# Ordering an eight-stage attention pipeline so that TensorE's fp32 instructions stand in four stretches a batch

## What is computed

```python
for W in (layer0, layer1):
    q = x @ Wq + bq;  k = ctx @ Wk + bk;  v = ctx @ Wv + bv
    w = softmax(q @ k.T / sqrt(512), axis=queries)
    y = w @ v + x
    x = (y - mean(y)) * rsqrt(var(y) + 1e-6) * gamma + beta
```

## Time and profile before

| | us |
|---|---|
| median of 3 runs | 1019.43 (1016.87 to 1020.06) |
| the profiled execution | 1016.79 |
| its span, first to last instruction | 1014.9 |
| mean granted TensorE clock | 0.995 |

### The profile page before, as it was taken

One profiled execution on the slowest core, in us unless ns is written; L12 is line 12 of the kernel. 1 busy time (PEld: TensorE's weight loads), 2 busy tenths in 40 slices (PEclk: granted clock), 3 DMA queues, 4 the chain that ended last, 5 costly groups with the idle time before them and its releaser, 6 DMA issues. The chain is left out here.

```text
span 1014.9 us, 23859 instructions
## 1 busy us (share of the span) xinstructions
PE 989.6 (98%) x6940; PEld 930.9 (92%) x6940; DVE 876.8 (86%) x2616; ACT 664.1 (65%) x1864; POOL 567.6 (56%) x522
## 2 busy tenths in 40 slices
PE   7989999999999999999999999999999999999985
PEld 6879999999999999999999999999999999999975
DVE  4788889988988998888988988898898889888867
ACT  2457767666766666776766676677667666667642
POOL 0134575556566555656555556655565665556574
PEclk9999999999999999999999999999999999999998
DMA  8653434544444454443454444345444445544101
GB/s 213 134 113 77 104 80 97 109 99 102 101 98 78 100 113 98 97 99 84 90 108 97 105 99 98 79 97 114 97 97 100 90 87 105 115 96 97 54 19 37
DMA packets 373958, 98.32 MB, mean 97 GB/s; under 512 B 308488, under 2 KB 357786, under 8 KB 373914
## 3 DMA queue, kind: packets, MB, share of 16 engines
q1 hardware_dynamic: 371370, 96.98, 44.2%
q10 hardware_dynamic: 2544, 0.80, 0.4%
HBM read 83.06 MB, written 14.68 MB: 96 GB/s over the span
## 5 line engine op out<-in xcount | busy, mean ns | idle before, releaser
L680 PE MATMUL oq_bank<-probs,raw 125*128 125x224 f32 x1488 | 302.8, 353 | 1.7 <-ACT probs L929 1.7
L680 PEld LDWEIGHTS oq_bank<-probs,raw 125*128 125x128 f32 x1488 | 272.2, 190 | 2.3 <-ACT probs L929 1.2
L913 ACT ACTIVATE probs<-probs,neg_max 125x224 f32<-125x224 f32 x378 | 177.8, 472 | 143.7 <-DVE neg_max L1194 143.6
L1521 POOL TENSOR_TENSOR psum<-probs 125x672 f32<-125x672 f32 x62 | 100.1, 1615 | 243.8 <-ACT probs L929 243.8
L656 PE MATMUL score_bank<-qT_hi,cT_hi 128*125 128x224 f32 x768 | 199.6, 286 | 3.9 <-ACT cT_hi L870 1.8
L657 PE MATMUL score_bank<-qT_hi,cT_lo 128*125 128x224 f32 x768 | 188.9, 273 | 0.0
L929 ACT ACTIVATE probs<-probs,rsum 125x224 f32<-125x224 f32 x378 | 150.8, 471 | 10.8 <-DVE rsum L1210 9.4
L1584 POOL TENSOR_TENSOR y_out<-z,gamma_row 112x512 f32<-112x512 f32 x62 | 93.9, 1536 | 113.9 <-ACT z L953 113.9
L656 PEld LDWEIGHTS score_bank<-qT_hi,cT_hi 128*125 128x125 f32 x768 | 145.2, 189 | 8.8 <-ACT cT_hi L870 3.4
L661 PE MATMUL score_bank<-qT_lo,cT_hi 128*125 128x224 f32 x768 | 147.1, 273 | 0.0
L657 PEld LDWEIGHTS score_bank<-qT_hi,cT_lo 128*125 128x125 f32 x768 | 145.4, 189 | 0.0
(11 more groups left out here) (136 smaller groups left out, 2038.9 us busy)
## 6 DMA issues: line engine op xcount, KB each, us to landing
raw<-in_ctx_dram SPq DMA_DIRECT2D x64, 375.0 KB
cb<-in_ctx_dram SPq DMA_DIRECT2D x248, 92.0 KB
x<-in_x_dram SPq DMA_DIRECT2D x32, 448.0 KB, 3.6
xb<-in_x_dram SPq DMA_DIRECT2D x124, 112.0 KB, 3.0
out_dram<-y_out SPq DMA_DIRECT2D x31, 448.0 KB, 6.7
cb<-in_ctx_dram SPq DMA_DIRECT2D x124, 3.5 KB
y<-in_L_xattn_Wq_dram SPq DMA_DIRECT2D x2, 512.0 KB, 5.5
Wq_next<-in_L_xattn_Wq_dram SPq DMA_DIRECT2D x2, 512.0 KB, 12.6
```

The source lines that it names most:

```text
L680: ins = nc.tensor.matmul(o, raw[0:MP, u.slot, c, cols], probs[0:MP, u.par4, c, :], start=(c == 0), stop=(c == MC - 1))
L913: ins = act.activation(probs[0:MP, u.par4, c, :], probs[0:MP, u.par4, c, :], ACT.Exp, bias=neg_max[0:MP, u.par4, c:c + 1], scale=-1.0, acc ...
```

## The change

Only the order of calls changes, on all five lists; no call is added or removed. TensorE's list, whole:

```diff
             def turn(i, j):
                 a, b = units(i, j)
+                spread_d(a(+0))
+                o_product(b(-1), 0)
                 score_product(a(+0), 0)
+                score_product(a(+0), 1)
+                transpose_x(b(+0), 0)
                 o_product(b(-1), 1)
-                transpose_x(b(+0), 0)
-                score_product(a(+0), 1)
+                transpose_x(b(+0), 1)
                 score_product(a(+0), 2)
-                transpose_x(b(+0), 1)
+                q_product(b(+0), 0)
                 pv_product(b(-1), 0)
-                q_product(b(+0), 0)
+                spread_d(b(+0))
+                q_product(b(+0), 1)
                 pv_product(b(-1), 1)
-                q_product(b(+0), 1)
-                o_product(a(+0), 0)
-                spread_d(b(+0))
                 score_product(b(+0), 0)
                 score_product(b(+0), 1)
+                o_product(a(+0), 0)
                 o_product(a(+0), 1)
                 score_product(b(+0), 2)
+                pv_product(a(+0), 0)
+                pv_product(a(+0), 1)
                 q_product(a(+1), 0)
-                pv_product(a(+0), 0)
-                spread_d(a(+1))
-                pv_product(a(+0), 1)
                 q_product(a(+1), 1)
-                o_product(b(+0), 0)
```

The fp32 stretches of a turn were o+r+transpose, transpose, o+spread, o+r, spread, o: six. They become spread+o, transpose+o+r+transpose, spread, o+o+r: four. VectorE's list, its first third (the calls behind are moved alike):

```diff
             def turn(i, j):
                 a, b = units(i, j)
+                score_max(b(-1), 2)
+                score_max(b(-1), 3)
+                ctxT_lo(a(+0), 0)
+                add_eps(b(-2))
+                turn_ctx(a(+0), 1)
                 shift(b(-2), 0)
-                score_max(b(-1), 2)
+                o_lo(a(-1), 0)
+                invert_sum(b(-1), 0)
                 shift(b(-2), 1)
-                dot(a(+0), 0)
-                dot(a(+0), 1)
+                o_lo(a(-1), 1)
                 residual(a(-1), 0)
                 residual(a(-1), 1)
-                score_max(b(-1), 3)
-                invert_sum(b(-1), 0)
-                o_lo(a(-1), 1)
+                ctxT_lo(a(+0), 1)
                 score_max(b(-1), 4)
+                turn_ctx(a(+0), 2)
                 score_max(b(-1), 5)
-                ctxT_lo(a(+0), 0)
                 add_pv(a(-1), 0)
+                add_pv(a(-1), 1)
+                half_moments(a(-1), 0)
+                invert_sum(b(-1), 1)
                 q_lo(a(+0), 0)
...
```

ScalarE's list, the calls around the second o_hi of a, and its end:

```diff
                 o_hi(a(-1), 1)
                 standardise(b(-2), 0)
+                ctxT_hi(a(+0), 1)
                 standardise(b(-2), 1)
-                ctxT_hi(a(+0), 0)
+                normalise(b(-1), 0)
+                ctxT_hi(a(+0), 2)
+                exps(b(-1), 1)
                 q_hi(a(+0), 0)
-                normalise(b(-1), 0)
-                exps(b(-1), 1)
                 normalise(b(-1), 1)
                 q_hi(a(+0), 1)
-                ctxT_hi(a(+0), 1)
-                o_hi(b(-1), 0)
+                d_out(a(+0))
+                standardise(a(-1), 0)
```

GpSimd's list and SP's:

```diff
+                inverse_deviation(a(-1))
                 sum_thirds(b(-1))
+                scale(a(-1), 0)
                 sum_two(b(-1))
-                inverse_deviation(a(-1))
                 sum_probs(b(-1))
-                scale(a(-1), 0)
-                add_beta(a(-1), 0)
-                scale(a(-1), 1)
                 sum_thirds(a(+0))
                 sum_two(a(+0))
+                scale(a(-1), 1)
+                add_beta(a(-1), 0)
+                sum_probs(a(+0))
+                inverse_deviation(b(-1))
                 add_beta(a(-1), 1)
-                inverse_deviation(b(-1))
-                sum_probs(a(+0))
                 scale(b(-1), 0)
...
                 if a(+0).later(1):
+                    load_xb(a(+0))
+                store(b(-3))
+                if a(-1).later(0):
+                    load_ctx(a(-1), 0)
+                    load_ctx(a(-1), 1)
+                if a(+0).later(1):
                     load_cb(a(+0))
                 if a(+1).later(1):
-                    load_xb(a(+1))
-                if a(+1).later(1):
                     load_x(a(+1))
-                if a(+0).later(0):
-                    load_ctx(a(+0), 0)
-                    load_ctx(a(+0), 1)
-                store(b(-2))
```

More of the change, by code:

```diff
@@ L767, in opening @@
                 spread_bk(1)
+                score_product(a1, 1)
                 transpose_x(b0, 0)
-                score_product(a1, 1)
+                transpose_x(b0, 1)
                 score_product(a1, 2)
-                transpose_x(b0, 1)
                 q_product(b0, 0)
+                spread_d(b0)
                 q_product(b0, 1)
-                o_product(a1, 0)
-                spread_d(b0)
                 score_product(b0, 0)
                 score_product(b0, 1)
+                o_product(a1, 0)
                 o_product(a1, 1)
                 score_product(b0, 2)
-                q_product(a2, 0)
                 pe.wait_ge(c_done, (LC + 1) * LAYERS)
                 pv_product(a1, 0)
-                spread_d(a2)
                 pv_product(a1, 1)
+                q_product(a2, 0)
                 q_product(a2, 1)
-                o_product(b0, 0)
             opening()
@@ L957, in turn @@
                 a, b = units(i, j)
-                ctxT_hi(a(-1), 2)
-                d_out(a(-1))
+                o_hi(b(-2), 0)
+                ctxT_hi(a(-1), 3)
                 if j is not None or i > 2:
-                    standardise(a(-2), 0)
                     standardise(a(-2), 1)
-                ctxT_hi(a(-1), 3)
+                xT_hi_part(b(-1), 0)
                 o_hi(b(-2), 1)
-                xT_hi_part(b(-1), 0)
-                exps(a(-1), 0)
                 xT_hi_part(b(-1), 1)
                 xT_hi_part(a(+0), 0)
+                exps(a(-1), 0)
                 exps(a(-1), 1)
@@ L1025, in _ @@
             q_hi(a1, 1)
+            ctxT_hi(a1, 2)
+            d_out(a1)
             turns(act, turn, 2)
@@ L1323, in turn @@
                 moments(a(-1), 1)
-                ctxT_lo(a(+0), 1)
+                add_eps(a(-1))
+                ctxT_lo(a(+0), 2)
+                turn_ctx(a(+0), 3)
+                shift(a(-1), 0)
                 q_lo(a(+0), 1)
[L1326 to L1329, removed]
                 shift(a(-1), 1)
-                ctxT_lo(a(+0), 2)
                 score_max(a(+0), 0)
-                turn_ctx(a(+0), 3)
@@ L1334, in turn @@
                 score_max(a(+0), 1)
                 ctxT_lo(a(+0), 3)
+                o_lo(b(-1), 0)
+                turn_x(a(+1), 0)
+                score_max(a(+0), 2)
                 xT_lo_part(b(+0), 0)
-                o_lo(b(-1), 1)
[L1338 to L1342, removed]
-                invert_sum(a(+0), 0)
-                score_max(a(+0), 5)
@@ L1345, in turn @@
-                xT_lo_part(b(+0), 1)
-                residual(b(-1), 1)
-                dot(b(+0), 0)
+                dot(b(+0), 0)
+                dot(b(+0), 1)
+                score_max(a(+0), 3)
+                residual(b(-1), 0)
+                xT_lo_part(b(+0), 1)
+                score_max(a(+0), 4)
+                score_max(a(+0), 5)
+                o_lo(b(-1), 1)
+                residual(b(-1), 1)
+                xT_lo_part(a(+1), 0)
+                invert_sum(a(+0), 0)
+                invert_sum(a(+0), 1)
@@ L1348, in turn @@
+                dot(a(+1), 0)
+                dot(a(+1), 1)
+                q_lo(b(+0), 0)
+                q_lo(b(+0), 1)
                 add_pv(b(-1), 0)
-                q_lo(b(+0), 0)
-                invert_sum(a(+0), 1)
-                dot(b(+0), 1)
+                turn_x(a(+1), 1)
                 half_moments(b(-1), 0)
-                xT_lo_part(a(+1), 0)
-                turn_x(a(+1), 1)
-                q_lo(b(+0), 1)
                 add_pv(b(-1), 1)
                 moments(b(-1), 0)
-                half_moments(b(-1), 1)
@@ L1431, in _ @@
             fold_c(1, 2)
+            turn_ctx(a1, 3)
             score_max(a1, 0)
-            turn_ctx(a1, 3)
             score_max(a1, 1)
             ctxT_lo(a1, 3)
+            turn_x(a2, 0)
+            score_max(a1, 2)
             xT_lo_part(b0, 0)
-            score_max(a1, 2)
+            dot(b0, 0)
+            dot(b0, 1)
             score_max(a1, 3)
-            turn_x(a2, 0)
+            xT_lo_part(b0, 1)
             score_max(a1, 4)
+            score_max(a1, 5)
+            xT_lo_part(a2, 0)
             invert_sum(a1, 0)
-            score_max(a1, 5)
-            xT_lo_part(b0, 1)
-            dot(b0, 0)
+            invert_sum(a1, 1)
+            dot(a2, 0)
+            dot(a2, 1)
             q_lo(b0, 0)
-            invert_sum(a1, 1)
-            dot(b0, 1)
-            xT_lo_part(a2, 0)
+            q_lo(b0, 1)
             turn_x(a2, 1)
-            q_lo(b0, 1)
-            o_lo(a1, 0)
             xT_lo_part(a2, 1)
@@ L1454, in _ @@
             score_max(b0, 1)
+            turn_ctx(a2, 0)
             Wv_lo_part(1)
-            turn_ctx(a2, 0)
             turns(dve, turn, 2)
```

14 lines of the change are left out of this document (5 added, 9 removed).

## The result

The changed kernel takes 1078.57 us (median, 1077.32 to 1079.16) against 1018.78, a ratio of 1.0586 with an interval of 1.0571 to 1.0602. I had said 1034, and 1014 to 1041. The direction is right, the size is not: 60 us, not 15.

The account below looks back on a forecast made before the run. TensorE's issue rate bounds the kernel; turns of 30.38 against 29.79 (7) and 30.41 against 29.915 (22) add 15.0 us, giving 1031.8, and 1034 with the median 2.6 us above the profiled execution. Range 1014 to 1041.

Parts of the forecast that it names:

- What bounds the kernel: TensorE runs at its own rate of issue, busy 989.6 of 1014.9 us; a new wait costs its full length.
- Fewer stretches: TensorE goes from six fp32 stretches a turn to four: 0.03 us a turn won, at most 0.18.
- The second rival: Each TensorE switch is worth the full 0.09 us, chain intact: 8.1 us less, 1011; chance 0.03.
- Loop waits: TensorE's two small waits in the loop, for oT_lo and before a score product, go: 0.13 us a turn won.
- The collision: GpSimd's scale holds VectorE's second residual about 1.05 us every turn; TensorE waits 0.62 to 0.65 at o_product(b, 0); chance 0.57.
- cb, "0 to 1 us a turn": In SP's queue cb starts near 8.6 us into the turn instead of 6.7; 0 to 1 us a turn, taken at nothing.
- The first: Rival: VectorE keeps its place between two residuals and GpSimd waits; the chain fits, 3.6 us less, 1016; chance 0.25.
- the third: Rival: without a collision, TensorE's wait on q_lo just misses by up to 0.15 us each turn, 1020; chance 0.11.
- The fourth: Rival: collision and late cb together, up to 1 us a turn more, near 1050; chance 0.04.
- Opening and tail: Both are reordered with the same work; put at 0, bound by 1 us each way.

Follow-up runs that it names:

- e8: The kernel before with ScalarE's ctxT_hi(a, 0) ahead of the two standardise(b-2), so GpSimd asks 0.4 us later: 1015.87 us, 0.9972.
- e6: The changed kernel with cb's transfers split around raw's second half, and ctxT_hi(a, 1) and normalise(b-1, 0) ahead of both standardise(b-2) on ScalarE: 1021.91 us, 1.0037.
- e5: The changed kernel with cb's transfers split, blocks 0 and 1 between the halves of raw, 2 and 3 behind them: 1041.89 us, 1.0228.
- e10: The kernel before with the changed kernel's order of SP's calls and nothing else: 1017.88 us, 0.9995.
- e2: The changed kernel with ctxT_hi(a, 1) and normalise(b-1, 0) ahead of the two standardise(b-2) on ScalarE, so GpSimd asks later: 1043.18 us, 1.0245.
- e4: The kernel before with o_lo(a-1, 1) ahead of the two residuals of a on VectorE, as in the changed kernel: 1027.46 us, 1.0094.
- e7: The kernel before with spread_d(a+1) moved to just ahead of o_product(b, 0), five fp32 stretches a turn instead of six: 1018.18 us, 1.0001.
- e9: The kernel of e6 with the opening's two transpose_x(b0) apart again, two score products between them: 1021.01 us, 1.0028.
- e1: The changed kernel with load_cb whole between the two halves of load_ctx in SP's list: 1050.97 us, 1.0322.
- e11: The kernel of e5 with VectorE's two residuals of a ahead of o_lo(a-1, 1), as in the kernel before: 1037.64 us, 1.0186.

## Why the prediction was right or wrong, step by step

**What bounds the kernel: right.** TensorE has no slack; 54.8 of the 62.2 us are in the turns, and the weight loads wait 46.8 us there at the one place named. Another 6.7 are the four stretches at the lower clock. My sum had no term for them: I had said that a new wait costs its full length, and four of these cost 1.67 us more.

**Fewer stretches, 0.03 us a turn: no gain.** 29.79 with six and with five, 29.81 with four. The second rival is dead. That agrees with my reading, that the delay behind an fp32 instruction is its own time, written to the next; the 0.015 that I still took was nothing.

**Loop waits, 0.13 a turn: about right.** e8 takes most of them away and wins 0.11 in undisturbed turns. In e6 they are gone too, but a few disturbed turns (mean 29.89, undisturbed ones 29.81) give it back.

**The collision: right in mechanism, place and size.** One residual of about 1.78 us in every turn, and GpSimd next each time: I had written 1.05 us of hold. By the Trainium skill, page "SBUF — State Buffer", section "Who interferes with whom", whoever issues first shuts the other out for that instruction. The trace agrees: between 909.11 and 911.60 above, both engines are slower than alone, the two scales with 3.46 us against 3.10 in the earlier trace rows, the two residuals with 2.49 against 1.34. Apart from cb it costs 0.65 us a turn in e5's mean; I had 0.62 to 0.65. In settled turns of the loop e5 takes 30.35 to 30.42 where I had 30.41, behind it 30.27 where I had 30.38, so there my stall was 0.1 too long.

**cb, "0 to 1 us a turn", taken at 0: this step failed.** Its first issue I had put 8.6 us into the turn, whose head is spread_d, 0.2 us ahead of o_product(b, 0), and it came nearly there. After, TensorE:

```profile
884.63 1.59 PE L680 MATMUL oq_bank<-probs,raw 125*128 125x224 f32 x7 [1.35 <-DVE qT_lo L1177]
```

and SP's queue:

```profile
893.22 3.33 SPq L388 DMA_DIRECT2D cb<-in_ctx_dram  x2
...
903.23 0.81 SPq L389 DMA_DIRECT2D cb<-in_ctx_dram  x1
```

893.22 - 884.63 = 8.6, and 8.8 with the spread. The user was wanted at 19.6. What I never put in the sum is how long twelve issues take: the last starts 903.23 - 893.22 = 10.0 us behind the first, and turn_ctx starts at 905.40, 12.2 us behind it. 8.8 + 12.2 = 21.0: 1.4 us late, which is the wait of 1.42. The trace of before had this length too. SP's queue before, the last issue of the turn of the earlier trace rows:

```profile
519.81 0.84 SPq L389 DMA_DIRECT2D cb<-in_ctx_dram  x1
```

and its user on VectorE:

```profile
521.88 0.59 DVE L1131 STREAM_TRANSPOSE t_bank<-cb 128x384 f32<-128x384 f32 x1 [0.17 <-DMA cb<-in_ctx_dram]
```

521.88 - 510.50 = 11.4 us from first issue to use, and a wait of 0.17 at its end: cb was already just in time. 8.6 + 11.4 = 20.0 against 19.6 would have told me that it is late, from before's rows alone. (The other 0.8 us of the 12.2 are the stretched first issues that e10 shows too; before's rows don't have them.) I read one row for the start of a load and none for its end.

**How the two add up.** My own numbers give it once cb is in. The late cb makes VectorE wait 41.2 / 21 = 1.96 us, of which the 0.7 us of idle that I had named covers a part: 1.26. The collision adds 1.05. The room ahead of o's weights was 1.05 - 0.62 = 0.43. Both: 1.26 + 1.05 - 0.43 = 1.88, measured 1.72 as wait at line 680 and as the difference of median turns; the mean's 1.91 has the lower clock in it. cb alone: 1.91 (40.2 / 21 in e2) - 0.7 - 0.43 = 0.78, measured 0.67 (0.74 by medians). The collision alone: 0.62, measured 0.65 (0.62). The turn quoted above has it in single steps: o_hi 0.65 late, plus 1.05, less 0.43, is 1.27; from the spread at 914.34 to the o at 915.75 it is 1.41, against 863.82 - 863.63 = 0.19 without a wait, 1.22 more. That the pieces fit within 0.2 us is an account and not a proof, but no other wait of size is left for it.

**The rivals.** The first is dead (e4), the second too (e7), the third had its condition but no case: without the collision q_lo just makes it (e6). The fourth was the right one, with a chance of 0.04 and 1050. It was too small in both: I bounded cb at 1 us, and it adds 31.79 - 30.54 = 1.25 to the collision, 0.23 of it by the lower clock; by median turns it is 31.53 - 30.43 = 1.10, and nothing softened it, since the room was spent.

**Opening and tail, 0, bound by 1 us each way: wrong.** 3.7 us each. In the opening it is in part the second transpose, 3.3 us, which e9 only moved. In the tail, 1.6 are the wait for q_lo once more, at the 30th o_product (1009.73), behind the 29 turns that I counted. The rest are after's waits on the matmuls (950 to 1080), of which these are the longest apart from those for q_lo (total, times, longest):

```profile
PE oq_bank L680 <- ACT probs L927: 1.7, 1, 1.7
PE oq_bank L636 <- DVE xT_lo L1146: 1.4, 1, 1.4
PE t_bank L590 <- ACT z L951: 1.3, 1, 1.3
PE score_bank L656 <- DVE neg_max L1194: 1.0, 1, 1.0
```

The kernel before waits for the same four there, only shorter (890 to 1015):

```profile
PE t_bank L590 <- DVE xT_lo L1146: 1.3, 1, 1.3
PE oq_bank L680 <- ACT probs L929: 0.8, 1, 0.8
PE t_bank L590 <- ACT z L953: 0.6, 1, 0.6
PE score_bank L656 <- DVE neg_max L1194: 0.4, 1, 0.4
```

5.4 against 3.1 us: the other 2 us or so. I had called it the same work; but where there is no next batch to fill in, a new order pays for each dependence whose ends it moves closer. That it is the order, and which call, was read from the rows and not tried.

**The sum with what was measured:** turns without either cause 29 x (29.89 - 29.90) = -0.5; the collision 29 x 0.65 = +18.9; cb on top of it 29 x 1.25 = +36.4; opening and tail +7.4. Together 62.2, the difference of the spans. It closes because each term is a difference of the same measured times, and is no check of the causes; of the 36.4, 6.7 are the lower clock.

## What to carry to other kernels

When a step that frees a buffer moves back, follow the transfer behind it to its last landing and not to its first issue, and set that against the moment its user is due; a wait of 0.1 or 0.2 us for a DMA in the old trace says that there is no slack. Two small delays that lean on the same room must be added before the room is taken off, once. A wait may cost more than its length: look at the granted clock behind it. And where GpSimd and VectorE meet over SBUF, look who triggers GpSimd: moving that trigger by a call or two cost nothing here, and even made the kernel before 0.28% faster.

## What the runs showed of the hardware that I had not expected

GpSimd was next each time it asked inside the first of the two queued residuals, VectorE instructions with two inputs in SBUF: in all 30 turns of the change, e1, e4 and e5, 14 of e11 and 11 of the kernel before. VectorE never kept its place, though its next instruction was ready.

The same twelve issues of cb are not of one length: the first two took 1.67 us in SP's queue before, behind the store, and 3.33 us after and 3.64 in e10, right behind the second half of raw; the later ones were about as long in all (0.81 to 0.84 for the last). Why was not tried. From the first issue to the use it makes 12.2 us instead of 11.4.

Alternating between fp32 and fp32r instructions on TensorE showed no cost: 59.58, 59.58 and 59.62 us for two turns with six, five and four fp32 stretches.

Behind four of the change's waits of about 2 us TensorE was granted 0.50 of its clock for 3.4 us, and each such stretch cost about 1.67 us beyond the wait.
